# First attention on raw transposed rows with scores scaled afterwards, first feed-forward's turns behind its projections, full-height bias products

## The reference

```python
x = x + tanh(g_xattn[0]) * L0_attention(layernorm(x), ctx)     # x 2 x 1024 x 256, ctx 2 x 77 x 128, one head
x = x + tanh(g_ffn[0])   * L0_ffn(layernorm(x))                # 256 -> 1024 -> 256
x = x + tanh(g_xattn[1]) * L1_attention(layernorm(x), ctx)     # 16 heads, then Wo and bo
x = x + tanh(g_ffn[1])   * L1_moe(layernorm(x))                # 8 experts, top 2, 512 slots each

def L0_attention(q, c):    # no scaling of the scores
    return softmax((q @ Wq + bq) @ (c @ Wk + bk).T) @ (c @ Wv + bv)
def L0_ffn(x):             # fix: round to multiples of 2**-8
    return fix(fix(pwl_gelu(fix(x @ w1 + b1))) @ w2 + b2)
def L1_moe(x):             # softmax gate, top 2, slots counted per expert, overflow dropped
    ...
```

## Time and profile before

| what | us |
|---|---|
| time, median of three runs (range) | 490.95 (490.82 to 492.32) |
| the profiled execution's own time | 491.95 |
| its span | 490.2 |
| PE busy | 454.8 (93%) |
| DVE busy | 370.4 (76%) |
| ACT busy | 258.6 (53%) |
| POOL busy | 145.6 (30%) |

### The profile page before, as it was taken

How to read it: one execution, slowest core, us unless ns; L and a number is a source line. 1 busy time by engine, 2 the same in 40 slices (tenths; PEclk the granted TensorE clock), 3 DMA queues, 4 the chain that set the end, 5 groups by cost and what they waited for, 6 DMA issues and landing times.

```text
span 490.2 us, 8549 instructions
## 1 busy us (share of the span) xinstructions
PE 454.8 (93%) x3226; PEld 395.9 (81%) x3226; DVE 370.4 (76%) x753; ACT 258.6 (53%) x416; POOL 145.6 (30%) x122
## 2 busy tenths in 40 slices
PE   6999999999998999998997499999999999999991
PEld 4787789798887888787886259989999999999991
DVE  4689998898988978899898966686757475757441
ACT  2577899697965664556554132463434344442220
POOL 3354100010002211222113063215263645445153
PEclk9999999999999999999999799999999999999997
DMA  7412200000000101312123341134363747461031
GB/s 243 136 43 60 82 1 2 0 1 1 1 0 1 45 1 44 117 57 87 45 86 127 126 125 55 23 130 136 98 162 96 170 96 195 86 174 20 3 48 16
DMA packets 37135, 36.06 MB, mean 74 GB/s; under 512 B 6442, under 2 KB 35942, under 8 KB 36966
## 3 DMA queue, kind: packets, MB, share of 16 engines
q1 hardware_dynamic: 30633, 27.65, 17.3%
q0 software_dynamic: 6144, 7.66, 9.1%
q10 hardware_dynamic: 317, 0.21, 0.1%
HBM read 27.69 MB, written 8.39 MB: 74 GB/s over the span
## 4 chain that ended last, share of the span: by engine, by line
PE 75%; DVE 15%; issue 4%; DMA 2%; ACT 1%; POOL 1%; ACTq 0%; DVEq 0%; POOLq 0%
PE PS L1489 19%; PE PS L1490 18%; PE PS L1491 18%; PE PS L1898 5%; PE PS L1509 2%; DVE nmaxC L1181 2%; PE PS L1844 2%; PE PS L1909 2%; DVE xn L1020 1%; DVE tmp L1184 1%; DVE st L993 1%; DMA tmp<-in_L_xattn_Wk 1%; PE PS L1546 1%; PE PS L1760 1%; DVE tmp L1231 1%
## 5 line engine op out<-in xcount | busy, mean ns | idle before, releaser
L1489 PE MATMUL PS<-w_hi,hT_hi 128*128 128x256 f32 x384 | 110.3, 287 | 0.8 <-DVE hT_lo L1161 0.6
L1490 PE MATMUL PS<-w_lo,hT_hi 128*128 128x256 f32 x384 | 108.6, 283 | 0.0
L1491 PE MATMUL PS<-w_hi,hT_lo 128*128 128x256 f32 x384 | 108.6, 283 | 0.0
L964 ACT ACTIVATE tmp<-PS,biasT 128x512 f32<-128x512 f32 (+1 forms) x80 | 43.8, 600 | 111.1 <-PE PS L1491 111.1
L673 POOL DMA_INDIRECT out<-tmp,dst_idx x32 | 56.1, 1754 | 98.6 <-DVE tmp L1445 91.8
L1489 PE MATMUL PS<-xT_hi,w_hi 128*128 128x512 f32 (+1 forms) x224 | 81.6, 364 | 1.1 <-DVE xT_lo L1028 1.1
L1490 PE MATMUL PS<-xT_lo,w_hi 128*128 128x512 f32 (+1 forms) x224 | 80.8, 361 | 0.0
L1491 PE MATMUL PS<-xT_hi,w_lo 128*128 128x512 f32 (+1 forms) x224 | 80.4, 359 | 0.0
L1489 PEld LDWEIGHTS PS<-w_hi,hT_hi 128*128 128x128 f32 x384 | 73.4, 191 | 4.1 <-issue 2.2
L1490 PEld LDWEIGHTS PS<-w_lo,hT_hi 128*128 128x128 f32 x384 | 73.5, 191 | 0.8
L1491 PEld LDWEIGHTS PS<-w_hi,hT_lo 128*128 128x128 f32 x384 | 73.5, 191 | 0.0
(11 more groups left out here) (254 smaller groups left out, 819.9 us busy)
## 6 DMA issues: line engine op xcount, KB each, us to landing
w_raw<-in_L_ffn_w SPq DMA_DIRECT2D x72, 256.0 KB, 3.0
residual<-in_x SPq DMA_DIRECT2D x4, 512.0 KB, 5.3
...
```

What stands on the lines that cost most here:

```text
L964: act.activation(gD[:, G % 2, f, 0:P * n], H[:, G % 2, f, 0:P * n], ACT.Gelu, bias=biasT[:, col:col + 1]).then_inc(e_gelu, 1)
L1489: pe.matmul(o, lh, rh, start=start, stop=False, skip_group_check=skip)
L1490: pe.matmul(o, lh, rl, start=False, stop=False, skip_group_check=skip)
L1491: return pe.matmul(o, ll, rh, start=False, stop=stop, skip_group_check=skip)
```

## The change

- **The host lays out** x also transposed (`xT`), the context, Wq of the first attention and Wo of the second transposed, and all biases as columns. The transpositions on TensorE of these five are gone, and so are ScalarE's copies of them; 2 MB more are loaded. ScalarE's queue issues nine transfers (four before), and SP's order is Wq transposed, then per chunk xT and x.
- **Scores from raw rows.** `centre_queries` on VectorE takes each row's mean off the transposed Wq, so that the mean of a row of x drops out of its scores. The scores are then products of the raw transposed rows, and `largest(c)` on VectorE scales them by the row's `rstd` and adds `beta`, the bias term, in four instructions, ahead of the maximum. `beta` is a product of full height. Rounds 0 to 3 have no `apply`, no `x_copy` and no turn any more. The keys' and both values' products stand ahead of the first scores.
- **Feed-forward turns.** `transpose_x` at g % 4 = 1, `output_bias`, `gate_weights` and `gate_constant` stand behind the step's `project` on TensorE, the last three one step later. `x_hi` goes from ScalarE's iteration g % 4 = 0 to 1, `x_rest` from 1 to 2.
- **Bias products.** The product that lays b2 into PSUM (L1722) has 128 rows, the unused ones zero, in place of 33.
- **Heads.** `heads_out` is gone; L1235's and L1240's work reads PSUM itself. GpSimd adds the scaled output bias to `xr` ahead of it, once per chunk (`add_output_bias`), and `rows_logits` adds the gate's constant. TensorE waits for both readers (`heads_read`) in place of `heads_out`.
- The split of the second Wq goes from VectorE to ScalarE and GpSimd, and the high parts of the first four feed-forward units are spread anew.

```diff
+                sp.dma_start(xT_raw(c), xT.rearrange("(k p) n -> p k n", p=P)[:, :, 512 * c:512 * c + 512]).then_inc(xT_loaded[c], 16)
                 sp.dma_start(xr[:, 4 * c:4 * c + 4, :], xf[:, 4 * c:4 * c + 4, :]).then_inc(x_loaded[c], 16)
...
+            sp.dma_start(wqT, WqT0.rearrange("(k p) d -> p k d", p=P)).then_inc(wq0_loaded, 16)
             load_x(0)
-            sp.dma_start(wq0_sb, Wq0.rearrange("(k p) e -> p k e", p=P)).then_inc(wq0_loaded, 16)
             load_x(1)
...
+            def add_output_bias(c):
+
+                pool.wait_ge(bo_ready, 1)
+                pool.wait_ge(xn_ready, round_of(2, c) + 1 - NC)
+                rows = xr[:, 4 * c:4 * c + 4, :]
+                pool.tensor_tensor(rows, rows, bcast(bo_bc[:, 0:D].unsqueeze(1), [P, 4, D]), ALU.add).then_inc(bias_added, 1)
...
                                    scale=2.0 ** -8).then_inc(hhi_ready, 1)
+                if g < NB_PAIRS and g % PAIRS == 2:
+                    x_rest(r)
                 if g % PAIRS == 2 and PAIRS < g < NB_PAIRS:
                     ffn_output(g // PAIRS - 1)
                 if g < NB_PAIRS:
-                    if g % PAIRS == 0:
+                    if g % PAIRS == 1:
                         x_hi(r)
-                    if g % PAIRS == 1:
-                        x_rest(r)
...
+            def centre_queries():
+
+                dve.wait_ge(wq0_loaded, 16)
+                for k in range(KD):
+                    ins = dve.bn_stats(wq_stats[:, k, :], wqT[:, k, :])
+                link(ins)
+                for k in range(KD):
+                    ins = dve.bn_aggr(wq_mean[:, k, :], wq_stats[:, k, :])
+                link(ins)
+                for k in range(KD):
+                    ins = dve.tensor_scalar(wqT[:, k, :], wqT[:, k, :], wq_mean[:, k, 0:1], None, ALU.subtract)
+                ins.then_inc(wq_centred, 1)
...
-            for c in range(NC):
...
+            def largest(c):
+
                 dve.wait_ge(a_scores, c + 1)
+                dve.wait_ge(rstd_ready, c + 1)
+                dve.wait_ge(kw_copied, 2)
                 if c >= 2:
-                    dve.wait_ge(a_exp, 4 * (c - 1))
-                dve.tensor_reduce(soft[:, c % 2, 0, :], SA[c % 2], AX_X, ALU.max, negate=True).then_inc(a_max, 1)
-                if c >= 1:
-                    stats(c + 2)
-                if 1 <= c < NC - 1:
-                    attended(c - 1)
+                    dve.wait_ge(a_tr, c - 1)
+                for i in range(4):
+                    dve.scalar_tensor_tensor(out=sA[:, c % 2, i, :], in0=SA[c % 2][:, i, :], scalar=rstd[:, c, i:i + 1],
+                                             in1=beta[:, c // (NC // 2), :], op0=ALU.mult, op1=ALU.add).then_inc(a_shift, 1)
+                dve.wait_ge(a_shift, 4 * (c + 1))
+                dve.tensor_reduce(soft[:, c % 2, 0, :], sA[:, c % 2, :, :], AX_X, ALU.max, negate=True).then_inc(a_max, 1)
+
+            def invert(c):
+
                 dve.wait_ge(a_exp, 4 * (c + 1))
                 recip_at.append(mark(dve.reciprocal(soft[:, c % 2, 2, :], soft[:, c % 2, 1, :])))
...
+            largest(0)
+            stats(2)
+            largest(1)
+            stats(3)
+            invert(0)
+            largest(2)
+            invert(1)
+            attended(0)
+            stats(NC)
+            largest(3)
+            apply(NC)
+            attended(1)
+            invert(2)
             x_lo(NC)
-            attended(NC - 2)
-            apply(NC + 1)
+            attended(2)
...
-            def heads_out(s):
+            def heads_residual(s):
                 dve.wait_ge(c_wo, s + 1)
-                dve.tensor_tensor(yC[:, s % 2, :], AT1[:, 0:D + NE], bo_bc[:, :], ALU.add).then_inc(c_wofree, 1)
-                dve.wait_ge(c_wofree, s + 1)
-
-            def heads_residual(s):
-                dve.scalar_tensor_tensor(out=xr[:, s, :], in0=yC[:, s % 2, 0:D], scalar=tg[:, 1:2], in1=xr[:, s, :],
+                dve.wait_ge(bias_added, s // 4 + 1)
+                dve.scalar_tensor_tensor(out=xr[:, s, :], in0=AT1[:, 0:D], scalar=tg[:, 1:2], in1=xr[:, s, :],
                                          op0=ALU.mult, op1=ALU.add).then_inc(x3_ready, 1)
...
             def heads_logits(s):
+                dve.wait_ge(c_wo, s + 1)
                 dve.wait_ge(lg_copied, s // 4 + 1)
-                dve.tensor_tensor(logits[:, s, :], yC[:, s % 2, D:D + NE], logits[:, s, :], ALU.add).then_inc(lg_added, 1)
+                dve.tensor_tensor(logits[:, s, :], AT1[:, D:D + NE], logits[:, s, :], ALU.add).then_inc(lg_added, 1)
...
+                dve.wait_ge(lg_copied, c + 1)
+                link(dve.tensor_tensor(logits[:, here, :], logits[:, here, :],
+                                       bcast(bo_bc[:, D:D + NE].unsqueeze(1), [P, 4, NE]), ALU.add))
...
                         attend_values(NC - 1)
-                    if g == PAIRS - 1:
+                if g == 2:
+                    pe.wait_ge(x1_ready, NT)
+                    keep_warm(6, 14)
+                if g >= LAG_B:
+                    project(g - LAG_B)
+                if g < NB_PAIRS:
+                    if g == PAIRS:
                         output_bias()
                     if g == PAIRS + 1:
                         pe.wait_ge(bo_ready, 1)
-                        pe.wait_ge(woT_copied, 1)
-                    if g == 2 * PAIRS - 1:
+                    if g == 2 * PAIRS:
                         pe.wait_ge(wg_ready, 2)
                         gate_weights()
                     if g == 2 * PAIRS + 1:
                         pe.wait_ge(wp_ready, 1)
-                    if g == 3 * PAIRS - 1:
+                    if g == 3 * PAIRS:
                         gate_constant()
                     if g == 3 * PAIRS + 1:
                         pe.wait_ge(wp_ready, 2)
                     if g % PAIRS == 1:
                         transpose_x(NC + g // PAIRS + 1)
-                if g == 2:
-                    pe.wait_ge(x1_ready, NT)
-                    keep_warm(6, 14)
-                if g >= LAG_B:
-                    project(g - LAG_B)
                 if g < NB_PAIRS and g % PAIRS == 2:
                     subtract_halves(NC + g // PAIRS + 1)
...
+            def heads_read(n):
+
+                pe.wait_ge(x3_ready, n)
+                pe.wait_ge(lg_added, n)
```

More of the change, by code:

```diff
@@ L153, in flamingo_gated_two_layers @@
         wqT = take(0, KD, D)
-        wq0_sb = take(0, KD, D)
         KT0 = take(0, KD, 2 * KEYS)
@@ L277, in flamingo_gated_two_layers @@
         wq0_loaded = sem("wq0_loaded")
-        b0_loaded = sem("b0_loaded")
+        bias_loaded = sem("bias_loaded")
+        xT_loaded = [sem(f"xT_loaded{c}") for c in range(NC)]
+        wq_centred = sem("wq_centred")
+        keys_psum = sem("keys_psum")
+        kw_psum = sem("kw_psum")
+        v0_psum = sem("v0_psum")
+        a_shift = sem("a_shift")
+        wq_rounded = sem("wq_rounded")
+        wq_split = sem("wq_split")
         v0_loaded = sem("v0_loaded")
@@ L435, in halves_of @@
         def halves_of(r):
+            if r < NC:
+                return 0
             if r >= NR or ROUNDS[r][0] < 2 or ROUNDS[r] == (2, 0):
@@ new lines, in _ @@
+            copy_turned(0)
+            exponentials(1)
+            exponentials(2)
+            copy_turned(1)
+            high_parts(0)
+            high_parts(1)
+            copy_turned(2)
+            act.wait_ge(query_loaded, 32)
+            act.activation(wq_hi[:, :, :], wq1_raw, ACT.Copy).then_inc(wq_rounded, 1)
+            exponentials(3)
+            x_hi(NC)
+            act.activation(small[:, 20:21], small[:, 16:17], ACT.Gelu)
+            copy_turned(3)
+            high_parts(2)
@@ L1551, in _ @@
             keep_warm(4, 6)
-            pe.wait_ge(ctx_loaded, 16 * N_CTX)
-            for b in range(2):
-                ins = pe.transpose(PS[:, 2, KEYS * b:KEYS * (b + 1)], ctx_sb[0:KEYS, b, :], ident[0:KEYS, 0:KEYS])
-            ins.then_inc(setup_psum, 1)
             def keys(bank, w):
@@ L1633, in output_bias @@
                 for k in range(KD):
-                    pe.matmul(T[:, 0, D:D + NE], ones_row[:, :], wg_raw[:, k, :], start=(k == 0), stop=(k == KD - 1))
-                for a in range(KD):
-                    for k in range(KD):
-                        ins = pe.transpose(T[:, 1, D * a + P * k:D * a + P * k + P], wo[:, k, P * a:P * a + P], ident[:, :])
+                    ins = pe.matmul(T[:, 0, D:D + NE], ones_row[:, :], wg_raw[:, k, :], start=(k == 0), stop=(k == KD - 1))
                 ins.then_inc(bo_psum, 1)
@@ L1980 @@
     nc = bacc.Bacc("TRN2", target_bir_lowering=False, num_devices=1)
+    x = np.asarray(inputs["x"])
+    laid = {"x": x, "xT": x.reshape(-1, x.shape[-1]).T, "ctxT": np.transpose(np.asarray(inputs["ctx_512"]), (2, 0, 1)),
+            "WqT0": np.asarray(inputs["L0_xattn_Wq"]).T, "WoT1": np.asarray(inputs["L1_xattn_Wo"]).T,
+            "bias_columns": np.concatenate([np.asarray(inputs[n]).reshape(-1, P) for n in _COLUMNS]).T}
```

(5 more changed lines are left out.)

362 lines of the change are left out of this document (145 added, 217 removed).

## The result

The changed kernel takes 505.74 us (median of 4 runs, 504.88 to 508.65), the kernel before 490.88 (490.72 to 492.32): 3.1% more, ratio 1.0306 with a 95% interval of 1.0259 to 1.0354. The forecast was 491.6, with a range up to 496. The profiled execution took 508.65, its span is 506.9 us.

What follows compares the result with a forecast made beforehand. Bounds taken: a chain through several engines in the front, mostly TensorE in the feed-forward, TensorE or VectorE in the heads. Front and feed-forward +3.8, heads -3.1: +0.7 on 490.95 gives 491.6 us; range 486.5 to 496.

Steps and rivals of the forecast that it cites:

- The first scores: Start of the first attention's scores: predicted at 17.1 us, bounds 14.5 and 19, against 16.01 before.
- The first `hidden`: Start of the feed-forward: predicted at 37.4 us, 20.3 after the first scores, against 41.21 before, a gain of 3.8.
- Then `apply(4)` 1.35: Step on VectorE between the first attention and the first `hidden`: `apply` for round 4 takes 1.35 us.
- `largest`: VectorE's step in the first attention: four instructions out of PSUM and a maximum, taken as 1.35 us, four times.
- `hidden(4)`: Second chunk's `hidden`: waits for ScalarE's `x_rest(5)`, starts at about 61.2 us against 60.89, TensorE idle 4 us.
- The bound I had set on this term, +1.5: Slower bound on the start of `hidden(4)`, where 0.3 us was predicted lost; the other bound was -3.8.
- my terms: Feed-forward: output bias +1.95, old turn waits gone -2.0, waits for late copies +3.8, full-height b2 product -0.25 us.
- rival 2: TensorE's clock falls to half rate after the gap ahead of `hidden(4)`, costing 3 us more: 494.6 us, chance 0.20.
- The heads: Heads: removing L1231's work from VectorE's chain gives -3.1 us, bounds -0.5 and -4.5.
- its three terms (4.7, 0.55, 1.05): Heads: 4.7 us gained from L1231, less 0.55 for TensorE's later releases and 1.05 for `rows_logits`' added instruction.
- Rivals 1 and 3: 1: ScalarE's copies in time, 488.4, chance 0.27 (full form 483.8, 0.05). 3: heads give only -0.5, 494.2, chance 0.14.
- the front's (a gain of 2 to 6): Bounds on how much earlier the first `hidden` starts: 2 and 6 us around the predicted 3.8.

Runs made afterwards that it cites:

- e3: The changed kernel with GpSimd's low parts of the first units held back until VectorE has written round 4's rows: 504.18 us.
- e14: The changed kernel with `x_hi` alone back in iteration g % 4 = 0, `x_rest` staying in g % 4 = 2: 503.33 us.
- e12: e9 with 14 keep-warm products (nobody reads them) in TensorE's gap ahead of `hidden(4)`: 499.37 us.
- e4: The kernel before with the change's heads part alone: 488.22 us.
- e9: The kernel before with the change's feed-forward order alone (TensorE's turns and small products behind projections, ScalarE's copies an iteration later): 501.44 us.
- e11: The kernel before with the b2 product at 128 rows in place of 33, and one more memset on VectorE: 490.62 us.
- e2: The changed kernel with the feed-forward's order as before on all engines, the new front kept: 498.49 us.
- e5: The changed kernel with e2 and e3 together (old feed-forward order, GpSimd's low parts held back): 492.75 us.
- e6: e5 with the fourth unit's low part on GpSimd back behind VectorE's first L1134, its high part ahead of the feed-forward: 491.16 us.
- e7: e6 with keep-warm products added where TensorE waits in the first attention: 490.17 us.
- e13: e7 with the turns of rounds 7 and 8 behind the projection, and SP's twelve placements ahead of the loads of units 2 and 3: 490.10 us.

## Why the prediction was wrong

**The first scores: right, in part by two errors that cancel.** 17.1 was predicted, 16.74 came. The bias product started at 10.99 and not at 10.1, because the second attention's keys, ahead of it, waited for their transfer until 9.80; KW took 1.82 and not 2.35. The table load behind its wait cost its own length, as I took it: it starts at 7.80 and the next instruction at 9.09.

```profile
7.80 1.28 ACT L729 ACT_TABLE_LOAD   x1 [7.80 <-PE PS L1555]
9.09 0.67 ACT L729 ACTIVATE tmp<-PS,biasT 128x154 f32<-128x154 f32 x2
```

The drain of 1.4 us that the Trainium skill puts behind such a load (page *ScalarE: Activation LUTs*, section "What ACT_TABLE_LOAD costs") is not in this trace either.

**The first `hidden`: wrong by 6.5 us, 43.86 instead of 37.4.** The step that failed is "Then `apply(4)` 1.35": it took 5.18, 3.8 more. I took its duration from a row in which GpSimd was nearly idle, and did not look at what GpSimd does beside it now. The trace of the kernel before had a sign of it, in rows that I did not use: one `apply` took 1.88 there, and it began within a subtraction of GpSimd:

```profile
28.90 1.27 POOL L599 TENSOR_TENSOR w_lo<-w_raw,w_hi 128x512 fp32r<-128x512 f32 x1
29.42 1.88 DVE L1020 TENSOR_SCALAR xn<-residual,mv,rstd 128x256 f32<-128x256 f32 x4
```

e3 gets the 1.37 back. Another 2.4 lie behind `apply`: from its end at 37.89 to the first `hidden` it is 6.0 us, where I had the turn, two copies and 0.35, 3.55. At half clock the turn takes 1.97 and the values product behind it 3.65, so TensorE is last there and not the copies (VectorE's ends at 42.24), and my sum had no values product. The chain ahead of `apply` was right to 0.6 us (15.97 from the first scores, 15.4 predicted). `largest` was right: 0.90 + 0.47 is 1.37, 1.35 was taken.

**`hidden(4)`: the mechanism was right and the size wrong.** I had TensorE idle for 4 us and `x_rest` as the last thing; it is 4.2 + 3.2, and the place is the one named. From the first `hidden` it is 28.3 us instead of my 23.8. Of the 4.5 missing, 1.4 come ahead of VectorE's first segment, which starts 7.5 behind the first `hidden` (51.33) and not 6.05: L987 takes 1.39 there beside GpSimd instead of 0.17. 2.0 are L1143 beside GpSimd (3.26 for 1.23). The last 1.1 is the step for ScalarE's chain: I let L891 wait for VectorE alone, and by the trace (below) ScalarE, ahead of it, waited 2.42 us for TensorE's `hidden(3)`, which was late by the wait at the subtraction and ran at half clock. e14 shows what that is worth: with `hidden(3)` early the same instruction comes 1.1 us sooner. A wait that I had put down as harmless on one engine held the chain that it waited for. The bound I had set on this term, +1.5, took in none of the three.

```profile
62.80 1.01 ACT L692 ACTIVATE xT_hi<-PS 128x1024 fp32r<-128x1024 f32 x1
...
68.98 1.27 ACT L821 ACTIVATE tmp<-PS,b_units 128x512 int32<-128x512 f32 x2 [2.42 <-PE PS L1489]
70.13 1.06 ACT L874 ACTIVATE hT_hi<-tmp 128x1024 fp32r<-128x1024 int32 x1
71.08 1.02 ACT L705 ACTIVATE xT_lo<-PS 128x1024 fp32r<-128x1024 f32 x1
```

**The feed-forward after it: 87.0 us from `hidden(4)` to the queries, 81.8 by my terms** (78.3 before, and 3.5 more). The windows from the one to the other, the kernel before first:

```profile
60.90:139.20 78.30, 76.31 (x487) 67.37 (x485) 69.32 (x76) 66.98 (x85) 1.38 (x1) 1.00 0.00 1
```

```profile
72.20:159.10 86.90, 81.60 (x494) 72.10 (x494) 69.08 (x73) 65.74 (x85) 4.56 (x2) 0.97 0.00 1
```

TensorE is idle for 5.30 us (86.90 less 81.60) where it was for 1.99, and busy for 5.29 more. The idle part is the waits for the copies (3.4 at the subtraction, 1.1 at `hidden`; I had 3.8 for both) and 0.9 at the turns, which now wait for the copies of the small products; the old waits of 1.0 did go. By my terms the idle time would be 3.8, so this part is 1.5 too small. Of the busy part 1.95 are `output_bias` (81.18 to 83.13), as I had it. The other 3.3 stand beside a granted clock of 0.97: the twelve products of `hidden(4)` alone start every 0.43 us and not every 0.23. My sum had nothing for that: it is rival 2.

**Rival 2 was right as a mechanism**, and was not a rival but a part: it held together with the forecast's waits. e12 prices it at 2.1 us for the gap ahead of `hidden(4)` by the medians (2.6 by the ratios, 2.9 by the traces), against the 3 that I gave. I had treated it as an either-or.

**The heads: right.** -3.1 predicted, 147.28 against 150.51 is -3.2 in the changed kernel, and -2.8 alone in e4. The sum is confirmed, its three terms (4.7, 0.55, 1.05) were not measured one by one. Rivals 1 and 3 are out: the copies were late, and the heads gave their gain.

**Where the 15 us are.** By experiments: the feed-forward's order alone is +10.7 (e9), the heads -2.8 (e4), full height -0.6 (e11). These leave 14.9 - 10.7 + 2.8 + 0.6 = +7.6 for the new front in their company; with the old order of the feed-forward the front costs 498.49 - 488.22 + 0.6, about +10.9 (e2 against e4; 9.4 by the ratios), of which 5.7 are the slow `apply` with what follows it (e5), 1.6 L1143 (e6) and 1.0 the clock (e7); by the ratios 4.4, 0.9 and 1.5. The two parts' losses overlap by some 2 to 3 us. About 2.5 us of the front remain after all that (e7 against e4, and the 0.6). The traces show where the front's gain is given back: in e7 the first `hidden` comes 3.3 us earlier than in the kernel before, but TensorE waits 0.89 us for VectorE's rows at the turn of round 5 and 2.42 at that of round 6, which starts at the same time as before (the kernel before first, then e7):

```profile
70.29 1.06 PE L1506 MATMUL PS<-ident,xn 128*128 128x128 f32 x8
```

```profile
70.29 1.07 PE L1506 MATMUL PS<-ident,xn 128*128 128x128 f32 x8 [2.42 <-issue]
```

e13 speaks against SP's placements as the cause. The trace points to VectorE, whose first segment does not come earlier: in each of these kernels one more of its instructions ahead of that segment is slow beside GpSimd's subtraction (L987 1.69 for 0.17 in e6, a cast 1.96 for 0.28 in e7, the casts 2.61 for 0.45 in e13). No run moved that subtraction, so this cause stays open.

**The range** was too narrow because each bound was set by itself, and the front's (a gain of 2 to 6) had no case for a slow instruction: three things that all made VectorE or ScalarE late (GpSimd beside it, a clock, an order) act on one chain.
